# Decoder layer on one core: the second pass with three x buffers, the next x transposed ahead of the output product, squares within softmax, 32-row scores, and half of K and V made in the first row

## Chip, cores and metric

The kernel runs on one core of a Trainium2 chip. The metric is the device time of the program in microseconds (us). The engines are TensorE (PE; its weight loads are shown apart as PEld), VectorE (DVE), ScalarE (ACT), GpSimd (POOL) and SyncE (SP), which issues most of the DMAs.

## What is computed

A post-norm decoder layer on x of 8 x 512 x 512, all in fp32:

```
x = layernorm(x + mamba(x))                      # first pass, not touched by the change
q = x @ Wq.T + bq ;  k = ctx @ Wk.T + bk ;  v = ctx @ Wv.T + bv      # ctx: 8 x 77 x 512, 16 heads of 32
s = where(mask, -inf, q k^T / sqrt(32)) ;  x = layernorm(x + softmax(s) v @ Wo.T + bo)
xp = x shifted down by one token (zero first)
r = sigmoid((mu_r x + (1-mu_r) xp) @ Wr) ;  kk = relu((mu_k x + (1-mu_k) xp) @ Wk2)**2
x = layernorm(x + r * (kk @ Wv2))
```

## The kernel before

The program has two passes. The first (the Mamba block) writes x1 to device memory. The second, `cross_attention_ffn_pass`, is what the change edits. It is written for each engine by hand: every engine has its own list of instructions, in the order in which the code stands, and waits on counting semaphores. No scheduler moves anything.

The second pass works on the batch in 8 "rows" b of 512 tokens (T = 512 columns, four blocks `tb` of 128 tokens, four blocks `kt` or `j` of 128 features). Two rows are in flight: in the program's row b, the attention of row b and the feed-forward part (FFN) of row b-1 are woven together. TensorE runs, in this order:

- `front(b)`: 16 transposes of x (L1016) into `x1t`, then the query product (L1003, 16 matmuls of 128x512), with copies by ScalarE between;
- `scores(b, tb)` (L1042), four matmuls of 128x308 for each of the four token blocks. One matmul covers four heads: `kbd` holds the keys of a row as a block-diagonal matrix, 128 features by 4 x 77 keys, zero outside the blocks. Block j goes to PSUM bank 4+j, and VectorE takes each bank as soon as it is full (scale, mask, L1322), then a maximum (L1328) and, once GpSimd has subtracted it (L1410) and ScalarE has taken exp (L1206), the sum and its reciprocal (L1306 to L1311); GpSimd multiplies (L1415);
- between the four score blocks: `x2_transposes(b-1)` of the normed row b-1, and the FFN's `ffn_k` (L1003 with `xk`), which needs `mix`, VectorE's blend of x with its shifted copy (L1299; `mixed`);
- `ffn_r`, then `ffn_v` (L1009), which waits for `squared`: GpSimd squares `kf` (L1427) after the last of the softmax;
- `attend(b)`: 64 transposes of the probabilities (L1080) with ScalarE's copies, the values (L1067: four heads side by side, each in its own 32 columns of the array), and the output product (L1095). VectorE adds it to x (L1366) and takes the statistics; ScalarE makes the reciprocal deviation (L1188 Ln, L1190 Exp), VectorE the norm (L1340).

`x1t` is one buffer with three names (`kf = ot = x1t`): the transposed x, the FFN's squares, and the attended values. x lies in two buffers `xn`, by the parity of the row. PSUM banks 0 to 3 go round for products that ScalarE takes (`a_bank`), banks 4 to 7 for those of VectorE (`v_bank`): a product waits until the fourth before it has been taken.

Before the first row, all keys (L1106, 32 matmuls of 128x308) and values (L1114, 32 matmuls of 77x512) of the 8 rows are made. That set-up waits for one semaphore of six loads, the identity matrix the last of them.

Of the kernel before, what the change touches and what calls it, by code (L numbers as in the profile page):

```python
# [819 lines left out]
def cross_attention_ffn_pass(nc, x1, ctx_t, attn_mask, pad_mask, wq, wk, wv, wo, bq, bk, bv, bo,  # L820
# [28 lines left out]
    SETUP_A, SETUP_V = KT * (NB // KB), NB  # L849
    FRONT, FFN, ATTEND = 2 * KT, 3 * KT, NH + KT  # L850
# [3 lines left out]
    def front_a(b):  # L854
        return SETUP_A if isinstance(b, int) and b == 0 else b * ROW_A + (SETUP_A - FFN)
# [4 lines left out]
    def scores_v(b):  # L860
        return SETUP_V if isinstance(b, int) and b == 0 else b * ROW_V + (SETUP_V - TT)
# [7 lines left out]
    with ctx:  # L869
# [36 lines left out]
        top, total, live = (sb(n, [P, TT, NH]) for n in ("top", "total", "live"))  # L906
# [5 lines left out]
        kv_loaded = sem("kv_loaded")  # L912
        w_loaded = sem("w_loaded")
        x_loaded = [sem(f"x_loaded{i}") for i in range(2)]
# [41 lines left out]
        @block.sync  # L956
        def _(sp):
            def load(b, par):
                for tb in range(TT):
                    sp.dma_start(xn[par][:, tb, :], x1[b, tb * P:(tb + 1) * P, :]).then_inc(x_loaded[par], 16)  # L960

            def store(b, par):
                for tb in range(TT):
                    sp.wait_ge(normed3, b * TT + tb + 1)
                    sp.dma_start(out[b, tb * P:(tb + 1) * P, :], xn[par][:, tb, :]).then_inc(stored, 16)

            for dst, src in kv_loads:
                sp.dma_start(dst, src).then_inc(kv_loaded, 16)
            load(0, 0)
            for dst, src in loads:  # L970
                sp.dma_start(dst, src).then_inc(w_loaded, 16)

            def row(b, par):

                if isinstance(b, int) and b == 0:
                    load(1, 1)
                    return
                store(b - 1, 1 - par)
                if not (isinstance(b, int) and b == NB - 1):
                    sp.wait_ge(stored, b * (16 * TT))  # L980
                    load(b + 1, 1 - par)

            rows(row, sp)
            store(NB - 1, (NB - 1) % 2)
            sp.wait_ge(stored, NB * TT * 16)

        @block.tensor
        def _(pe):
            pe.wait_ge(kv_loaded, 16 * len(kv_loads))

# [29 lines left out]
            def front(b, par):  # L1020
                a = front_a(b)
                pe.wait_ge(x_loaded[par], (b - par) * (8 * TT) + 16 * TT)
                for kt in range(KT):
                    transposed(a, kt, xn[par])

                pe.wait_ge(a_taken, a + KT)
                for j in range(KT):
                    product_a(a, KT + j, lambda kt: wq_s[:, kt, j * P:(j + 1) * P], lambda kt: x1t[:, kt, :])

            def x2_transposes(b, a, par):  # L1030
                pe.wait_ge(normed2, b * TT + TT)
                for kt in range(KT):
                    transposed(a, kt, xn[par])
# [22 lines left out]
            def attend(b):  # L1056
# [30 lines left out]
                values(KT - 1, n)  # L1087

# [12 lines left out]
            for half in range(NB // KB):  # L1101
                for j in range(KT):
                    i = half * KT + j
                    a_bank(i + 1)
                    for kt in range(KT):
                        m = nc.tensor.matmul(ps[:, j, 0:KB * NK], wk_s[:, kt, j * P:(j + 1) * P],  # L1106
                                             ctx_s[:, kt, half * KB * NK:(half + 1) * KB * NK],
                                             start=(kt == 0), stop=(kt == KT - 1))
                    m.then_inc(a_filled, 1)

            for i in range(NB):
                v_bank(i + 1)
                for kt in range(KT):
                    m = nc.tensor.matmul(ps[0:NK, 4 + i % 4, :], ctx_s[:, kt, i * NK:(i + 1) * NK], wv_s[:, kt, :],  # L1114
                                         start=(kt == 0), stop=(kt == KT - 1))
                m.then_inc(v_filled, 1)
# [3 lines left out]
            def row(b, par):  # L1120
# [17 lines left out]
                if not first:  # L1138

# [3 lines left out]
                    ffn_v(b - 1, scores_v(b) + TT * KT)  # L1143
                attend(b)

            rows(row, pe)
            x2_transposes(NB - 1, LAST_A, (NB - 1) % 2)
# [8 lines left out]
        def _(act):  # L1156
            act.wait_ge(kv_loaded, 16 * len(kv_loads))
            act.wait_ge(zeroed, 2)
            for half in range(NB // KB):
                for j in range(KT):  # L1160
                    act.wait_ge(a_filled, half * KT + j + 1)
                    for i in range(HB):
                        r0 = i * DK
                        s = nc.scalar.activation(
                            kbd[r0:r0 + DK, half * KB:(half + 1) * KB, j, i * NK:(i + 1) * NK],
                            ps[r0:r0 + DK, j, 0:KB * NK].rearrange("p (b n) -> p b n", b=KB),
# [343 lines left out]
```

## Time and profile before

| | us |
|---|---|
| median of 3 runs | 2757.8 (2755.11 to 2761.13) |
| the profiled execution, its own time | 2748.2 |
| its span, first to last instruction | 2746.3 |
| set-up of the second pass starts on TensorE | 1854.42 |
| first output product (row 0) starts | 1959.38 |
| last output product (row 7) starts | 2661.13 |

TensorE is busy for 91% of the span, VectorE 71%, GpSimd 64%, ScalarE 53%. Most of VectorE's and GpSimd's time is the first pass. A matmul of fp32 shows as two instructions in the trace, each with its weight load, so 16 matmuls are "x32". The busy time of a group counts up to the end of its last instruction, which lies beside the start of the next group; the pace is read from one start to the next.

### The profile page before, as it was taken

How to read it: one execution, taken by the hardware profiler on the slowest of the kernel's cores; microseconds unless marked ns; L12 is line 12 of the kernel's file. 1: busy time of each engine (PE TensorE's matmuls, PEld its weight loads, DVE VectorE, ACT ScalarE, POOL GpSimd, SP SyncE). 2: the span in 40 equal slices, each digit the busy share in tenths (PEclk: the TensorE clock that was granted, in tenths of full speed). 3: DMA queues.
4: the chain of work that ended last, by engine and by line, in shares of the span. 5: the costliest groups of instructions: out<-in, count | busy, mean ns of one | idle time of the engine just before them, and what ended most of it. 6: DMA issues, size and time to landing. Idle time of an engine off the chain costs nothing. (4 is left out here: it accounts for less than half of the span.)

```text
span 2746.3 us, 37070 instructions
## 1 busy us (share of the span) xinstructions
PE 2496.2 (91%) x14848; PEld 1466.2 (53%) x14848; DVE 1963.0 (71%) x2273; ACT 1447.0 (53%) x2151; POOL 1765.5 (64%) x974
## 2 busy tenths in 40 slices
PE   7899999999999999999999997869799999999996
PEld 3566556556556555655565655534444444444443
DVE  3888997997998898888899798741456356446452
ACT  3576567567567557656657746513343343433432
POOL 0799889889889879878988988950333133124120
PEclk9999999999999999999999999989899999999998
DMA  3656666656766756665666675652000000000000
GB/s 136 154 124 138 175 136 135 181 129 134 185 131 140 186 111 149 140 166 130 148 176 133 128 169 124 135 135 109 0 0 31 31 0 31 31 25 7 31 16 16
DMA packets 99771, 292.11 MB, mean 106 GB/s; under 512 B 9360, under 2 KB 43664, under 8 KB 76944
## 3 DMA queue, kind: packets, MB, share of 16 engines
q0 software_dynamic: 27648, 167.78, 31.3%
q1 hardware_dynamic: 71952, 121.95, 12.6%
q8 instruction: 118, 1.93, 0.3%
q14 instruction: 53, 0.43, 0.1%
HBM read 104.89 MB, written 17.04 MB: 44 GB/s over the span
## 5 line engine op out<-in xcount | busy, mean ns | idle before, releaser
L781 POOL TENSOR_TENSOR mamba_ring<-mamba_ring,mamba_c_row 128x1024 f32<-128x1024 f32 x512 | 1286.9, 2586 | 177.7 <-DVE mamba_ring L664 176.3
L664 DVE TENSOR_TENSOR_SCAN mamba_ring<-mamba_ring,ps 128x512 f32<-128x512 f32 x1024 | 1177.0, 1201 | 149.0 <-PE ps L341 139.6
L535 ACT ACTIVATE mamba_ring<-mamba_delta,mamba_a_neg 128x512 f32<-128x512 f32 x1024 | 666.1, 712 | 468.3 <-DMA mamba_ring<-mamba_ring 335.2
L341 PEld LDWEIGHTS ps<-mamba_diag_b,mamba_v_t 64*128 64x128 f32 x8192 | 505.8, 190 | 365.9 <-issue 243.3
L341 PE MATMUL ps<-mamba_diag_b,mamba_v_t 64*128 64x128 f32 x8192 | 600.8, 288 | 89.0 <-DVE mamba_ring L664 87.9
L251 PE MATMUL ps<-mamba_xt,mamba_wu 128*128 128x512 f32 x512 | 254.9, 626 | 24.9 <-DMA mamba_wu<-w_u 12.9
L309 PE MATMUL ps<-mamba_xt,mamba_wres 128*128 128x512 f32 x512 | 256.5, 624 | 0.0
L1404 POOL TENSOR_TENSOR xf_xn<-xf_xn,xf_bo_s 128x512 f32<-128x512 f32 x32 | 39.7, 1274 | 333.1 <-PE xf_ps L1016 333.1
L364 PE MATMUL ps<-mamba_ident,mamba_ring 128*128 128x128 f32 x1536 | 189.8, 280 | 30.0 <-DMA mamba_ring<-mamba_ring 27.7
L1410 POOL TENSOR_TENSOR xf_pr<-xf_pr,xf_top 128x1232 f32<-128x1232 f32 x32 | 71.9, 2248 | 214.2 <-DVE xf_top L1328 214.2
L797 POOL DMA_DIRECT2D mamba_ring<-mamba_ring x192 | 174.4, 909 | 43.7 <-POOL mamba_ring L781 35.4
L642 DVE SCALAR_TENSOR_TENSOR mamba_u<-ps,mamba_wcv,mamba_u 128x511 f32<-128x511 f32 (+2 forms) x192 | 141.6, 738 | 73.1 <-ACT mamba_u L500 70.4
L364 PEld LDWEIGHTS ps<-mamba_ident,mamba_ring 128*128 128x128 f32 x1536 | 171.1, 144 | 42.3 <-DMA mamba_ring<-mamba_ring 22.4
L392 PE MATMUL ps<-mamba_wout,mamba_u 128*128 128x512 f32 x352 | 176.6, 621 | 0.0
L1003 PE MATMUL xf_ps<-xf_xk,xf_wkf 128*128 128x512 f32 x256 | 124.9, 646 | 28.3 <-DVE xf_xk L1299 21.6
L251 PEld LDWEIGHTS ps<-mamba_xt,mamba_wu 128*128 128x128 f32 x512 | 90.8, 195 | 108.6 <-issue 99.6
L773 POOL TENSOR_TENSOR mamba_v<-mamba_delta,mamba_u 128x512 f32<-128x512 f32 x64 | 96.2, 1503 | 62.2 <-ACT mamba_delta L517 62.2
L309 PEld LDWEIGHTS ps<-mamba_xt,mamba_wres 128*128 128x128 f32 x512 | 88.8, 193 | 76.1 <-issue 63.7
L500 ACT ACTIVATE mamba_u<-ps,mamba_bcv,mamba_wcv 128x512 f32<-128x512 f32 x64 | 49.5, 773 | 145.1 <-PE ps L251 145.1
L1322 DVE SCALAR_TENSOR_TENSOR xf_pr<-xf_ps,xf_mask 128x308 f32<-128x308 f32 x128 | 56.2, 471 | 96.7 <-PE xf_ps L1042 95.1
L1003 PE MATMUL xf_ps<-xf_x1t,xf_wq 128*128 128x512 f32 x256 | 113.8, 603 | 7.6 <-ACT xf_x1t L1176 7.6
L1232 ACT COPY xf_pt<-xf_ps 77x512 f32<-77x512 f32 x128 | 64.6, 593 | 105.9 <-PE xf_ps L1080 105.7
(111 smaller groups left out, 3050.7 us busy)
## 6 DMA issues: line engine op xcount, KB each, us to landing
mamba_ring<-mamba_ring POOLq DMA_DIRECT2D x128, 1024.0 KB, 7.6
mamba_c_row<-c_rows SPq DMA_DIRECT2D x32, 1024.0 KB, 10.2
mamba_ring<-mamba_ring POOLq DMA_DIRECT2D x64, 512.0 KB, 6.8
mamba_wu<-w_u SPq DMA_DIRECT2D x64, 256.0 KB, 3.5
mamba_wres<-w_res SPq DMA_DIRECT2D x64, 256.0 KB, 3.1
mamba_xt<-x_t SPq DMA_DIRECT2D x8, 1024.0 KB, 9.3
mamba_xres<-x SPq DMA_DIRECT2D x32, 256.0 KB, 9.1
x<-mamba_xres SPq DMA_DIRECT2D x32, 256.0 KB, 3.3
```

The costliest lines, as they stand in the source:

```text
L251: m = nc.tensor.matmul(ps[:, bank, :], wu[n % 2][:, kt, :], xt[b % 2][:, kt, :], start=(kt == 0), stop=(kt == KT - 1))
L309: m = nc.tensor.matmul(ps[:, BANK_B, :], wres[g % 2][:, kt, :], xt[b % 2][:, kt, :], start=(kt == 0), stop=(kt == KT - 1))
L341: m = nc.tensor.matmul(ps[:, 2 * s + i, tb * P:(tb + 1) * P], v_t[g % 2][i * H:(i + 1) * H, tb * P:(tb + 1) * P], diag_b[i * H:(i + 1) * H ...
L364: m = nc.tensor.matmul(ps[:, y_bank(g), tb * P:(tb + 1) * P], ring[:, r, i, tb * P:(tb + 1) * P], ident[:], is_transpose=True, start=(k == ...
L392: m = nc.tensor.matmul(ps[:, bank, :], u[b % 2][:, d, tb * P:(tb + 1) * P], wout[:, d, :], start=(d == 0), stop=(d == MOST[tb] - 1))
L535: a = nc.scalar.activation(ring[:, q % NR, i, :], delta[:, d, :], ACT.Exp, scale=a_neg[:, d, 2 * k + i:2 * k + i + 1])
L642: nc.vector.scalar_tensor_tensor(u[b % 2][:, j, lag:], ps[:, bank, 0:T - lag], wcv[:, j, TP - lag:TAPS - lag], u[b % 2][:, j, lag:], ALU.m ...
L664: m = nc.vector.tensor_tensor_scan(ring[:, r, i, :], ring[:, r, i, :], both[:, bass.ds(i, T, 2)], 0.0, ALU.mult, ALU.add)
L773: nc.gpsimd.tensor_tensor(v[:].rearrange("p b i t -> p i b t"), in_blocks(delta[:, d, :]), in_blocks(u[b % 2][:, d, :]), ALU.mult).then_in ...
L781: nc.gpsimd.tensor_tensor(ring[:, q % NR], ring[:, q % NR], c_row[:, 2 * k:2 * k + 2, :], ALU.mult).then_inc(c_done, 1)
L797: nc.gpsimd.dma_start(dst, src, accum_op=ALU.add).then_inc(merged[p], 16)
L1003: m = nc.tensor.matmul(ps[:, i % 4, :], lhs_t(kt), rhs(kt), start=(kt == 0), stop=(kt == KT - 1))
```

## The change

In the second pass alone:

- `xn` has three buffers (row b in `b % 3`), so x of row b+1 is there early; `kf = ot` is a buffer apart from `x1t`.
- `x1_transposes(b+1)` are issued within `attend(b)`, after the last values and before the output product.
- The query product of row b is split: two blocks, then the transposes of the normed row b-1, then the other two.
- Score blocks: 16 matmuls of K=32, 77 columns each, in the four 32-row tiles of the array, on plain keys `k_t` in place of the block-diagonal `kbd`. Head i of each block of four goes to bank 4+i, and the bank is full only when all four j are done.
- FFN products `ffn_k` 0, 1 after score block 0, 2, 3 after block 1; blocks 2 and 3 follow one another.
- GpSimd's squares lie within the softmax; VectorE's two `mix` are one place earlier; `live` and its product are one operation (L1340 of the new code).
- ScalarE loads one table for Ln and Exp ahead of its use, after the sigmoids; the deviation of the FFN's norm is made after the first four copies of `attend`.
- The keys of batch rows 4 to 7 are made between the score blocks of the first row, the values of 4 to 7 after them. The keys wait for three loads only.
- In the tail `ffn_k` waits for the first four of `mixed`, not for all.

The core of the diff:

```diff
-        kbd = sb("kbd", [P, NB, KT, HW])
+        k_t = sb("k_t", [P, NB, KT, NK])
-        xn = [sb(f"xn{i}", [P, TT, DM]) for i in range(2)]
+        xn = [sb(f"xn{i}", [P, TT, DM]) for i in range(3)]
-        kf = ot = x1t
+        kf = ot = sb("kf", [P, KT, T])
...
             def scores(b, tb):
                 v = scores_v(b)
                 if tb == 0:
-                    pe.wait_ge(a_taken, front_a(b) + 2 * KT)
+                    pe.wait_ge(a_taken, q_a(b, KT - 1) + 1)
                 for j in range(KT):
-                    v_bank(v + (tb * KT + j + 1))
-                    nc.tensor.matmul(ps[:, 4 + j, 0:HW], qt[:, j, tb * P:(tb + 1) * P], kbd[:, b, j, :],
-                                     start=True, stop=True).then_inc(v_filled, 1)
+                    for i in range(HB):
+                        r0 = i * DK
+                        if j == 0:
+                            v_bank(v + (tb * HB + i + 1))
+                        m = nc.tensor.matmul(ps[:, 4 + i, j * NK:(j + 1) * NK],
+                                             qt[r0:r0 + DK, j, tb * P:(tb + 1) * P], k_t[r0:r0 + DK, b, j, :],
+                                             start=True, stop=True, tile_position=(r0, 0))
+                        if j == KT - 1:
+                            m.then_inc(v_filled, 1)
...
                 values(KT - 1, n)
+                if b + 1 < NB:
+                    x1_transposes(b + 1)
...
+            for j in range(KT):
+                k_context(0, j)
+            pe.wait_ge(v_loaded, 16 * len(v_loads))
+            for i in range(VB):
+                v_context(i)
             pe.wait_ge(w_loaded, 16 * len(loads))
-            def row(b, par):
-                first = isinstance(b, int) and b == 0
-                front(b, par)
+            def row(b):
+                q_product(b, 0)
+                q_product(b, 1)
+                if b > 0:
+                    x2_transposes(b - 1)
+                q_product(b, 2)
+                q_product(b, 3)
                 scores(b, 0)
-                if not first:
-                    a = front_a(b) + FRONT
-                    x2_transposes(b - 1, a, 1 - par)
-                scores(b, 1)
-                if not first:
+                if b > 0:
+                    a = ffn_a(b - 1)
                     pe.wait_ge(mixed, (b - 1) * (2 * KT) + KT)
                     ffn_k(a, 0)
                     ffn_k(a, 1)
-                scores(b, 2)
-                if not first:
+                else:
+                    k_context(1, 0)
+                    k_context(1, 1)
+                scores(b, 1)
+                if b > 0:
                     ffn_k(a, 2)
                     ffn_k(a, 3)
+                else:
+                    k_context(1, 2)
+                    k_context(1, 3)
+                scores(b, 2)
                 scores(b, 3)
...
+                else:
+                    for i in range(VB, NB):
+                        v_context(i)
                 attend(b)
...
             x2_transposes(NB - 1)
-            pe.wait_ge(mixed, NB * (2 * KT))
+            pe.wait_ge(mixed, NB * (2 * KT) - KT)
             for j in range(KT):
                 ffn_k(LAST_A, j)
+            pe.wait_ge(mixed, NB * (2 * KT))
```

The order on TensorE, from the output product of one row to the FFN's `ffn_v` in the next; `xf_xn` transposed is x or the normed row, `xf_kbd` and `xf_k_t` are the keys. Before:

```order
L1095 MATMUL xf_ps<-xf_wo,xf_x1t 128x512 x16
L1016 MATMUL xf_ps<-xf_ident,xf_xn 128x128 x16
L1003 MATMUL xf_ps<-xf_x1t,xf_wq 128x512 x16
L1042 MATMUL xf_ps<-xf_kbd,xf_qt 128x308 x4
L1016 MATMUL xf_ps<-xf_ident,xf_xn 128x128 x16
L1042 MATMUL xf_ps<-xf_kbd,xf_qt 128x308 x4
L1003 MATMUL xf_ps<-xf_xk,xf_wkf 128x512 x8
L1042 MATMUL xf_ps<-xf_kbd,xf_qt 128x308 x4
L1003 MATMUL xf_ps<-xf_xk,xf_wkf 128x512 x8
L1042 MATMUL xf_ps<-xf_kbd,xf_qt 128x308 x4
L1003 MATMUL xf_ps<-xf_wr,xf_xr 128x512 x16
L1009 MATMUL xf_ps<-xf_wvf,xf_x1t 128x512 x16
```

And in the changed kernel, from the transposes that now stand ahead of the output product:

```order
L1014 MATMUL xf_ps<-xf_ident,xf_xn 128x128 x16
L1117 MATMUL xf_ps<-xf_wo,xf_kf 128x512 x16
L1000 MATMUL xf_ps<-xf_x1t,xf_wq 128x512 x8
L1014 MATMUL xf_ps<-xf_ident,xf_xn 128x128 x16
L1000 MATMUL xf_ps<-xf_x1t,xf_wq 128x512 x8
L1059 MATMUL xf_ps<-xf_k_t,xf_qt 128x77 x16
L1000 MATMUL xf_ps<-xf_xk,xf_wkf 128x512 x8
L1059 MATMUL xf_ps<-xf_k_t,xf_qt 128x77 x16
L1000 MATMUL xf_ps<-xf_xk,xf_wkf 128x512 x8
L1059 MATMUL xf_ps<-xf_k_t,xf_qt 128x77 x32
L1000 MATMUL xf_ps<-xf_wr,xf_xr 128x512 x16
```

The x transposes moved ahead of the output product, the normed ones into the query product, and two score blocks now stand together (x32) with nothing between.

GpSimd in one row, where `xf_top` is subtracted, `xf_total` multiplied, and the buffer of the squares is `xf_x1t` before:

```order
L1410 TENSOR_TENSOR xf_pr<-xf_pr,xf_top 128x1232 x2
L1415 TENSOR_TENSOR xf_pr<-xf_pr,xf_total 128x1232
L1410 TENSOR_TENSOR xf_pr<-xf_pr,xf_top 128x1232
L1415 TENSOR_TENSOR xf_pr<-xf_pr,xf_total 128x1232
L1410 TENSOR_TENSOR xf_pr<-xf_pr,xf_top 128x1232
L1415 TENSOR_TENSOR xf_pr<-xf_pr,xf_total 128x1232 x2
L1427 TENSOR_TENSOR xf_x1t<-xf_x1t 128x512 x4
```

The same engine and place in the changed kernel, with the squares on `xf_kf`:

```order
L1444 TENSOR_TENSOR xf_pr<-xf_pr,xf_top 128x1232 x2
L1449 TENSOR_TENSOR xf_pr<-xf_pr,xf_total 128x1232
L1455 TENSOR_TENSOR xf_kf<-xf_kf 128x512 x2
L1444 TENSOR_TENSOR xf_pr<-xf_pr,xf_top 128x1232
L1449 TENSOR_TENSOR xf_pr<-xf_pr,xf_total 128x1232
L1444 TENSOR_TENSOR xf_pr<-xf_pr,xf_top 128x1232
L1449 TENSOR_TENSOR xf_pr<-xf_pr,xf_total 128x1232
L1455 TENSOR_TENSOR xf_kf<-xf_kf 128x512 x2
L1449 TENSOR_TENSOR xf_pr<-xf_pr,xf_total 128x1232
```

All four squares now end one multiplication before the softmax does, in place of after it.

## Rows read from the trace of the kernel before

**Rows 1.** Windows: PE, PEld, DVE, ACT, POOL busy us; granted clock, DMA share, GB/s.
```profile
2250.00:2350.00 100.00, 94.97 (x325) 48.03 (x324) 52.17 (x91) 39.02 (x62) 28.01 (x17) 0.98 0.06 22
```

**Rows 2.** Timeline of TensorE, one steady row; start, us, operands, count [idle before].
```profile
2260.57 14.00 PE L1095 MATMUL xf_ps<-xf_wo,xf_x1t 128*128 128x512 f32 x32
...
2274.45 1.97 PE L1016 MATMUL xf_ps<-xf_ident,xf_xn 128*128 128x128 f32 x16
2277.25 14.00 PE L1003 MATMUL xf_ps<-xf_x1t,xf_wq 128*128 128x512 f32 x32 [0.83 <-ACT xf_x1t L1176]
2292.03 2.34 PE L1042 MATMUL xf_ps<-xf_kbd,xf_qt 128*128 128x308 f32 x8 [0.78 <-ACT xf_qt L1182]
2294.21 1.91 PE L1016 MATMUL xf_ps<-xf_ident,xf_xn 128*128 128x128 f32 x16
...
2301.28 8.83 PE L1003 MATMUL xf_ps<-xf_xk,xf_wkf 128*128 128x512 f32 x16 [3.09 <-DVE xf_xk L1299]
...
2335.19 14.00 PE L1009 MATMUL xf_ps<-xf_wvf,xf_x1t 128*128 128x512 f32 x32 [0.33 <-POOL xf_x1t L1427]
2349.03 3.66 PE L1080 MATMUL xf_ps<-xf_ident,xf_pr 128*77 128x128 f32 x32
...
2360.29 14.00 PE L1095 MATMUL xf_ps<-xf_wo,xf_x1t 128*128 128x512 f32 x32
```

**Rows 3.** Timeline of TensorE in the first pass: the two-tile products.
```profile
99.30 2.12 PE L341 MATMUL ps<-mamba_diag_b,mamba_v_t 64*128 64x128 f32 x32
...
704.86 1.16 PE L341 MATMUL ps<-mamba_diag_b,mamba_v_t 64*128 64x128 f32 x16
705.95 1.98 PE L309 MATMUL ps<-mamba_xt,mamba_wres 128*128 128x512 f32 x4
```

**Rows 4.** Timeline of VectorE and ScalarE in the steady row.
```profile
2278.83 1.28 ACT L1190 ACT_TABLE_LOAD   x1
...
2280.36 3.02 DVE L1340 TENSOR_SCALAR xf_xn<-xf_xn,xf_mv,xf_rstd 128x512 f32<-128x512 f32 x4 [1.90 <-ACT xf_rstd L1190]
...
2311.57 1.62 DVE L1322 SCALAR_TENSOR_TENSOR xf_pr<-xf_ps,xf_mask 128x308 f32<-128x308 f32 x4
```

**Rows 5.** Groups by line, second pass: busy, mean ns of one, idle before.
```profile
L1328 DVE TENSOR_REDUCE xf_top<-xf_pr 128x16 f32<-128x1232 f32 x32 | 46.0, 1436 | 1.1
L1410 POOL TENSOR_TENSOR xf_pr<-xf_pr,xf_top 128x1232 f32<-128x1232 f32 x32 | 71.9, 2248 | 214.2 <-DVE xf_top L1328 214.2
...
L1427 POOL TENSOR_TENSOR xf_x1t<-xf_x1t 128x512 f32<-128x512 f32 x32 | 32.4, 1039 | 71.1 <-ACT xf_x1t L1210 71.1
```

**Rows 6.** Timeline of TensorE from the set-up through the first row.
```profile
1854.42 18.63 PE L1106 MATMUL xf_ps<-xf_pt,xf_xr 128*128 128x308 f32 x64 [19.97 <-DMA xf_ident<-ident]
1872.89 27.63 PE L1114 MATMUL xf_ps<-xf_xk,xf_pt 128*77 128x512 f32 x64
...
1904.22 14.00 PE L1003 MATMUL xf_ps<-xf_x1t,xf_wq 128*128 128x512 f32 x32 [1.95 <-ACT xf_x1t L1176]
...
1946.05 5.74 PE L1080 MATMUL xf_ps<-xf_ident,xf_pr 128*77 128x128 f32 x32 [12.43 <-POOL xf_pr L1415]
...
1959.38 14.00 PE L1095 MATMUL xf_ps<-xf_wo,xf_x1t 128*128 128x512 f32 x32
```

**Rows 7.** DMA view and SyncE timeline: the key bias, last of the three loads for the keys.
```profile
xf_bk<-bk SPq DMA_DIRECT2D x1, 2.0 KB, 8.4
...
1841.99 0.42 SPq L968 DMA_DIRECT2D xf_bk<-bk  x1
```

**Rows 8.** Timelines of TensorE, VectorE and ScalarE after the last row.
```profile
2661.13 14.00 PE L1095 MATMUL xf_ps<-xf_wo,xf_x1t 128*128 128x512 f32 x32
...
2693.28 16.20 PE L1003 MATMUL xf_ps<-xf_xk,xf_wkf 128*128 128x512 f32 x32 [6.72 <-DVE xf_xr L1299]
...
2690.49 2.73 DVE L1299 SCALAR_TENSOR_TENSOR xf_xr<-xf_x2t,xf_omr,xf_xr 128x512 f32<-128x512 f32 x4
...
2739.75 1.28 ACT L1190 ACT_TABLE_LOAD   x1
```

More of the change, by code:

```diff
@@ L905, in cross_attention_ffn_pass @@
         tick = sb("tick", [P, 1])
-        top, total, live = (sb(n, [P, TT, NH]) for n in ("top", "total", "live"))
+        top, total = (sb(n, [P, TT, NH]) for n in ("top", "total"))
         st6, mv, rstd = sb("st6", [P, TT, 6]), sb("mv", [P, TT, 2]), sb("rstd", [P, TT])
@@ L1233, in attend @@
                         n += 1
+                    if j == 0 and before:
+                        rstd_ffn(b - 1)
                     if j >= 1:
@@ L1267, in _ @@
-            rows(row, act)
+                take_q(b, 0)
+                take_q(b, 1)
+                if b > 0:
+                    take_x2(b - 1)
+                    scale_x2(b - 1, xk, muk, range(KT))
+                take_q(b, 2)
+                if b > 0:
+                    scale_x2(b - 1, xr, mur, (0, 1))
+                take_q(b, 3)
+                if b > 0:
+                    scale_x2(b - 1, xr, mur, (2, 3))
+                else:
+                    take_context(1)
+                for tb in range(TT):
+                    exp(b, tb)
+                    if b > 0 and tb < 2:
+                        take_k(ffn_a(b - 1), 2 * tb)
+                        take_k(ffn_a(b - 1), 2 * tb + 1)
@@ L1268, in _ @@
+                if b > 0:
+                    for tb in range(TT):
+                        take_r(ffn_a(b - 1), tb)
+                    exp_tables()
+                attend(b, b > 0)
+            act.wait_ge(k_loaded, 16 * len(k_loads))
+            take_context(0)
+            act.wait_ge(w_loaded, 16 * len(loads))
+            act.wait_ge(consts, 5)
+            act.wait_ge(zeroed, 1)
+            exp_tables()
+            for b in range(NB):
+                row(b)
             rstd_of(z2_stats, 2 * TT, mv, rstd, rstd2_ln, rstd2, NB - 1)
-            take_x2(LAST_A)
@@ L1384, in _, with row @@
-            rows(row, dve)
-            last = (NB - 1) % 2
-            norms(NB - 1, last, mv, rstd, rstd2, normed2)
+            def row(b):
+                if b > 0:
+                    norms(b - 1, mv, rstd, rstd2, normed2)
+                softmax(b, b == 0)
+                if b > 0:
+                    ffn_out(b - 1, ffn_a(b - 1), scores_v(b) + TT * KT)
+                    norms(b - 1, gmv, grstd, rstd3, normed3)
+                attention_out(b)
+            for b in range(NB):
+                row(b)
@@ L1424, in squares @@
-            def squares(b, a):
-                for j in range(KT):
-                    pool.wait_ge(a_taken, a + (KT + j + 1))
-                    nc.gpsimd.tensor_tensor(kf[:, j, :], kf[:, j, :], kf[:, j, :], ALU.mult).then_inc(squared, 1)
-            def row(b, par):
-                first = isinstance(b, int) and b == 0
-                prepare(b, par)
-                softmax(b)
-                if not first:
-                    squares(b - 1, front_a(b) + FRONT)
-            rows(row, pool)
@@ new lines, in squares @@
+            def squares(b, js):
+                for j in js:
+                    pool.wait_ge(a_taken, ffn_a(b) + (KT + j + 1))
+                    nc.gpsimd.tensor_tensor(kf[:, j, :], kf[:, j, :], kf[:, j, :], ALU.mult).then_inc(squared, 1)
+            for b in range(NB):
+                prepare(b)
+                centre(b, 0)
+                centre(b, 1)
+                weigh(b, 0)
+                if b > 0:
+                    squares(b - 1, (0, 1))
+                centre(b, 2)
+                weigh(b, 1)
+                centre(b, 3)
+                weigh(b, 2)
+                if b > 0:
+                    squares(b - 1, (2, 3))
+                weigh(b, 3)
@@ L1440, in decoder_layer @@
+            squares(NB - 1, range(KT))
 def decoder_layer(nc, t, out):
```

292 lines of the change are left out of this document (131 added, 161 removed).

## The prediction

> **What bounds the kernel now.** I read the windows first: in 100 us of the steady part TensorE is busy for 94.97, VectorE for 52, GpSimd for 28 [rows 1]. So a row of the second pass lasts as long as TensorE's work plus its few waits, and another engine matters only where one of these waits ends on it. From one output product to the next a row takes 2360.29 - 2260.57 = 99.7 us [rows 2]; over the seven from row 0 to row 7 it is (2661.13 - 1959.38) / 7 = 100.25 [rows 6, 8].
>
> TensorE's timeline shows what the 99.7 hold [rows 2]. The big products pace at 13.8 us per 16 matmuls (2335.19 to 2349.03). The waits are: the copy of x before the query product (0.83 idle; with the pipeline's tail about 1.06 from the last transpose issued); the last copy of q before the scores (0.78, in the same way 1.05); VectorE's `mix` before `ffn_k` (3.09 idle, with the tail 3.3); the squares before `ffn_v` (0.33, some 0.5). The `mix` wait costs a second time: the 8 matmuls behind it take 8.83 against half of the 14.00 of a product of 16, because the granted clock falls to half behind that wait (0.98 on average over the window, rows 1); that is 1.8 us. A wait of 1.95 with no such loss stands before the first query product, which takes 14.00 [rows 6].
>
> **The change, part by part, in the steady row.**
> x of the next row is transposed before the output product, into a buffer of its own. The 16 transposes cost the same (1.97 with the tail, 1.74 of issue), but ScalarE's copies lie under 13.8 us of product: minus 1.06.
>
> `mix`: the transposes of the normed row now come 6.9 us into the query product instead of behind the first score block. Is the normed row ready? The norm starts at 2280.36, 6.0 behind the output product's end near 2274.4 [rows 2, 4]; 1.28 of that is a table load, now gone [rows 4]. Its four operations took 3.02 beside GpSimd's bias addition. That addition now lies under the output product, so I take 1.9 (the 2.7 of four larger VectorE operations with GpSimd idle, rows 8, is an upper bound). So ready at 4.7 + 1.9 = 6.6, against 6.9: no wait, or up to 0.9 if it stays at 3.0. From there to the blended `xk` is 7 us of copies, scalings and mix, at t = 14; `ffn_k` starts at 13.8 + 1.7 + 1.05 + 1.1 = 17.6. Minus 3.3 and minus the 1.8 of clock.
>
> Score blocks. Before, one takes 2.18 (2292.03 to 2294.21, rows 2), 2.07 of it products. The new one has 32 instructions of 77 columns. Its columns alone would need a quarter of the time of 308, divided once more among the tiles, so weight loads set the pace. The nearest rows are the two-tile products of the first pass, 64-row tiles and 128-column weights [rows 3]: 16 instructions take 1.09 to the next product's start, and 16 more add 2.12 - 1.16 = 0.96. That is 0.12 us for each pair side by side. If four row tiles load side by side as those two do, a block is 8 such steps, like those 16 instructions: 1.1. If only two do, it is 16 steps, 2.05; if none do, 32 steps, 3.84. I take 1.1: the tiles are apart in rows and banks as those two are, and the four value products of four heads (L1067) already run side by side in four column tiles. Four blocks: 4 x (1.1 - 2.1) = -4.
>
> A rule of the Trainium skill speaks against this (TensorE: Matmul & The Clock Gate, LDWEIGHTS): a weight load takes as long for 32 rows as for 128, since its columns count, 107 ns for 128 columns at 1.2 GHz. As an estimate from that page, 32 loads in turn would be 3.4 us a block, and nothing would be gained; the same page (Part 3) lets loads of different row groups overlap. The trace agrees with the first on the step's length (0.12) and with the second for two tiles; no row has four row tiles.
>
> A new wait: blocks 2 and 3 stand together, and a bank is full only at the block's end. Block 3 begins when VectorE has taken all four banks of block 2: 0.3 until the first starts, 1.6 for the four [rows 4], 0.1 back. Three quarters of block 3 remain behind the last bank, so it loses some 1.8. VectorE is free in time: block 1's maximum (1.44, rows 5) and shares end about 2 us before block 2 is full. Plus 1.8.
>
> Squares: they follow GpSimd's third multiplication. Counting on from block 2's take (t = 35.5): maximum 37, shares 39.8, block 3's take and maximum 42.9, subtraction 2.25 [rows 5], shares 45.5, multiplication 47.8, two squares of 1.04 [rows 5] 49.9. `ffn_v` is due at 36.5 + 13.8 = 50.3. Minus 0.5, but the margin is 0.4.
>
> ScalarE's reciprocal deviation within `attend` puts 0.6 among copies that TensorE waits for: plus 0.3. The wait of 1.05 before the scores stays. The other edits (`live`, three x buffers, loads two rows earlier) touch engines that wait anyway: nothing; without that cover `live` would be worth 1 us per block.
>
> The new row: five products 69.0, two sets of transposes 3.5, `attend` 11.3 (2349.03 to 2360.29) + 0.3, scores 4.4, waits 1.05 + 1.8 = 91.3. Seven rows, the last without transposes: 639.1 - 1.7 = 637.4 against 701.75: **minus 64**.
>
> **Set-up and row 0.** The keys need the first three loads: the last of them lands at 1841.99 + 8.4 = 1850.4 [rows 7], 3.8 before TensorE's start at 1854.42 [rows 6]. Half the keys: 64 instructions took 18.47, and at the 2.07 / 8 us of a score product of the same shape they would take 16.5, so 2.0 were lost to the clock's start at half: 8.2 + 2.0, to 1860.8. Four values at 27.6 / 8 = 3.43: 1874.5. From there to the query product 3.9 before, now with a table load of 1.28 ahead of the copies: 1879.7 (1904.22 before). Query product and wait to 1894.5; three score blocks and the other keys (2 x 4.1) to 1906. Here ScalarE can take exp 0 only after all the keys, at 1906; VectorE holds the take of block 2 behind its shares, until 1909.3. Block 3 ends at 1912, the first value product waits for a bank until about 1915, and by the 3.09 wait's example runs 1.8 slower: to 1930.6. `attend` and transposes 13.0: the output product starts at 1943.6 instead of 1959.38: **minus 15.7**. Of the 22 us of moved keys and values, most returns into this row, whose softmax left 12.43 idle [rows 6].
>
> **Tail.** `ffn_k` no longer waits for the four `xr` mixes, 2.7; two table loads (1.28 each, before norm 2 and before norm 3) are gone [rows 4, 8]: **minus 5.2**.
>
> Sum: 64.3 + 15.7 + 5.2 = 85, against a profiled execution of 2748.2 (span 2746.3 and 1.9 around it): 2663. The runs' median is 9.6 above that execution, so I forecast 2757.8 - 85 = **2672**.
>
> **Rivals.**
> Two tiles at a time (0.14): 32 blocks x 0.95 = 30 us back: 2702. For it: the only row-tile rows have two. Against it: the four column tiles.
> The clock falls in the thin stretch of blocks 2 and 3 too (0.13). For it: 2 us of tiled work around a 1.8 wait. Against it: a wait of 1.95 cost nothing [rows 6]. 1.8 to 3 in each of 7 rows: 2685 to 2693.
> `ffn_v` waits for squares, or the transposes for the norm (0.10): margins of 0.4 and 0.3. One to three us a row: 2679 to 2693.
> The tiles run in turn (0.05), the other side. Blocks of 3.84 give back 88: 2760, no change. The point is a block of 1.1 + 85 / 32 = 3.76; past it the kernel is slower, and if the half-busy array lets the clock fall as well, each block costs up to 7.7 and the time goes well over 2800. I give 0.02 to no change and 0.03 to slower.
> All as forecast (0.55): 2660 to 2686 for the small unknowns of 0 to 2 us a row. The rest (0.03) is faster, with blocks under 0.9 or a shorter row 0.
>
> **Numbers.** Time 2672. The range reaches from 2656 up to two tiles at a time, 2705; what lies outside is the tiles in turn and the ends. A measurement of this kernel tells some 0.2% (5.5 us) from no change. Faster than that: 0.95; within: 0.02; slower: 0.03.
>
> **What would show it.** A start-to-start pitch of 91 us between output products; no idle before the `xk` products and 7.0 us for their 8 matmuls; a score block of 1.1; one wait on VectorE's take (L1356) before block 3; no wait before `ffn_v`; the first output product near 1944 and TensorE's last score block of row 0 followed by a wait for a bank. The forecast is wrong if the weight loads of four row tiles don't overlap, since a third of the gain rests on that, or if the waits moved onto VectorE are longer than its own row's slack.

## The result, and the profile after

The changed kernel takes **2682.17 us** in the median (2679.95 to 2683.65, 4 runs) against 2758.72 for the kernel before beside it (2755.11 to 2761.13, 4 runs): a ratio of **0.9744**, 95% interval 0.9717 to 0.9771 (the ratio on record; these two medians alone give 0.9723). The forecast was 2672.

The profiled execution took 2683.6 (span 2681.8), 20.6 more than the 2663 of the forecast's sum. The first pass, which the change leaves alone, ran 4.0 longer in this execution (1840.65 against 1836.64 to the issue of its last four stores). I measure the second pass from there: 841.15 us against 909.68, **68.5 less**. That is 8 less than the 76.5 between the two medians, since the runs of the kernel before took some 10 us longer than its profiled execution (2748.2); in which part of the program these 10 us lie isn't on record.

| us | before | forecast | after |
|---|---|---|---|
| second pass to the first output product | 122.74 | 106.96 | 110.86 |
| seven rows | 701.75 | 637.4 | 651.18 |
| from the last output product on | 85.19 | 80.0 | 79.12 |

TensorE's timeline of a steady row, which answers to [rows 2]:

```profile
2231.60 13.90 PE L1117 MATMUL xf_ps<-xf_wo,xf_kf 128*128 128x512 f32 x32
2245.33 7.03 PE L1000 MATMUL xf_ps<-xf_x1t,xf_wq 128*128 128x512 f32 x16
2252.20 1.91 PE L1014 MATMUL xf_ps<-xf_ident,xf_xn 128*128 128x128 f32 x16
2253.95 7.03 PE L1000 MATMUL xf_ps<-xf_x1t,xf_wq 128*128 128x512 f32 x16
2261.75 1.13 PE L1059 MATMUL xf_ps<-xf_k_t,xf_qt 32*128 32x77 f32 x32 [0.78 <-ACT xf_qt L1200]
2262.82 7.13 PE L1000 MATMUL xf_ps<-xf_xk,xf_wkf 128*128 128x512 f32 x16
...
2278.00 1.13 PE L1059 MATMUL xf_ps<-xf_k_t,xf_qt 32*128 32x77 f32 x32
2279.69 2.27 PE L1059 MATMUL xf_ps<-xf_k_t,xf_qt 32*128 32x77 f32 x32 [0.55 <-DVE xf_pr L1356]
2281.88 15.70 PE L1000 MATMUL xf_ps<-xf_wr,xf_xr 128*128 128x512 f32 x32
2297.42 13.90 PE L1007 MATMUL xf_ps<-xf_wvf,xf_kf 128*128 128x512 f32 x32
```

Of the four waits of [rows 2], those for x, for `mix` and for the squares are gone; the one for q stays at 0.78. A score block takes 1.06 from start to start (2261.75 to 2262.82), half of the 2.18 before. The new wait is the 0.55 before block 3, and block 3 itself is stretched, since its banks come free one by one: from block 2's start to `ffn_r` it is 3.88 instead of 2 x 1.06, so 1.76 are lost. What the sum did not count stands in the next line: the 16 matmuls (x32) of `ffn_r` take 15.70, where `ffn_v` behind them takes 13.90. Windows around that place (PE, PEld, DVE, ACT, POOL busy; granted clock; DMA share; GB/s):

```profile
2278.00:2282.00 4.00, 3.45 (x66) 2.94 (x66) 2.81 (x5) 0.71 (x2) 3.10 (x3) 1.00 0.02 4
2282.00:2286.00 4.00, 4.00 (x6) 1.70 (x7) 3.93 (x8) 1.23 (x1) 3.27 (x2) 0.57 0.00 0
2286.00:2297.00 11.00, 11.00 (x27) 4.79 (x27) 6.93 (x9) 4.20 (x5) 9.89 (x6) 1.00 0.00 1
```

TensorE is busy throughout the second window, but at a granted clock of 0.57, near the lower of its two levels (1.2 of 2.4 GHz). In two of the seven rows the loss starts sooner, within block 3:

```profile
2465.30 3.02 PE L1059 MATMUL xf_ps<-xf_k_t,xf_qt 32*128 32x77 f32 x32 [0.55 <-DVE xf_pr L1356]
2468.24 16.57 PE L1000 MATMUL xf_ps<-xf_wr,xf_xr 128*128 128x512 f32 x32
```

The other engines in the first row shown, VectorE and GpSimd, against [rows 4, 5]:

```profile
2249.99 1.92 DVE L1377 TENSOR_SCALAR xf_xn<-xf_xn,xf_mv,xf_rstd 128x512 f32<-128x512 f32 x4 [0.60 <-ACT xf_rstd L1208]
...
2255.68 2.74 DVE L1331 SCALAR_TENSOR_TENSOR xf_xk<-xf_x2t,xf_omk,xf_xk 128x512 f32<-128x512 f32 x4 [3.38 <-ACT xf_xk L1220]
2231.84 4.94 POOL L1437 TENSOR_TENSOR xf_xn<-xf_xn,xf_bo_s 128x512 f32<-128x512 f32 x4 [29.27 <-PE xf_ps L1014]
...
2292.79 2.04 POOL L1455 TENSOR_TENSOR xf_kf<-xf_kf 128x512 f32<-128x512 f32 x2
```

The norm takes 1.92 (3.02 before); GpSimd's bias addition now lies 13 us ahead of it, and e3 below shows what it costs when the two overlap; the table load of [rows 4] before it is gone; `mix` ends at 2258.4, 4.4 before its reader. The last squares end at 2294.83, 2.6 before `ffn_v`.

TensorE in row 0, against [rows 6]:

```profile
1883.72 16.98 PE L1000 MATMUL xf_ps<-xf_x1t,xf_wq 128*128 128x512 f32 x32 [3.23 <-ACT xf_x1t L1195]
...
1916.46 3.13 PE L1059 MATMUL xf_ps<-xf_k_t,xf_qt 32*128 32x77 f32 x32 [3.03 <-DVE xf_pr L1356]
1922.06 16.55 PE L1045 MATMUL xf_ps<-xf_xk,xf_pt 128*77 128x512 f32 x32 [2.47 <-DVE xf_pr L1356]
```

The query product starts 43.07 into the second pass; the forecast's 1879.7 is 43.06. It then takes 16.98, 3.0 longer than the 14.00 of [rows 6].

### The profile page after: what moved, and what is told of

It is laid out like the page before. It is cut to its first block and busy times, and to the rows that moved or that the text cites. A ratio compares the mean times of both kernels' runs of the same rounds, so it can differ in the third digit from the quotient of the medians.

```text
span 2681.8 us, 38529 instructions
## 1 busy us (share of the span) xinstructions
PE 2475.2 (92%) x15616; PEld 1461.2 (54%) x15616; DVE 1942.1 (72%) x2241; ACT 1403.5 (52%) x2106; POOL 1755.6 (65%) x973
## 5 line engine op out<-in xcount | busy, mean ns | idle before, releaser
L1403 DVE TENSOR_TENSOR xf_xn<-xf_xn,xf_ps 128x512 f32<-128x512 f32 x32 | 21.2, 663 | 158.3 <-PE xf_ps L1117 158.3
L773 POOL TENSOR_TENSOR mamba_v<-mamba_delta,mamba_u 128x512 f32<-128x512 f32 x64 | 95.6, 1494 | 58.0 <-ACT mamba_delta L517 58.0
L1000 PE MATMUL xf_ps<-xf_wr,xf_xr 128*128 128x512 f32 x256 | 125.4, 653 | 0.0
L500 ACT ACTIVATE mamba_u<-ps,mamba_bcv,mamba_wcv 128x512 f32<-128x512 f32 x64 | 49.5, 773 | 145.0 <-PE ps L251 145.0
L1225 ACT ACTIVATE xf_pr<-xf_pr 128x1232 f32<-128x1232 f32 x32 | 39.3, 1230 | 162.1 <-POOL xf_pr L1444 162.1
L1000 PE MATMUL xf_ps<-xf_xk,xf_wkf 128*128 128x512 f32 x256 | 115.3, 605 | 4.1 <-DVE xf_xk L1331 4.1
```

The costliest lines, as they stand in the source:

```text
L1000: m = nc.tensor.matmul(ps[:, (a + i) % 4, :], lhs_t(kt), rhs(kt), start=(kt == 0), stop=(kt == KT - 1))
```

## The experiments

Each was timed in three rounds beside the kernel before (e1, e2, e5 and e8 on one chip, median 2751.5; e3, e4, e6 and e7 on one, 2751.0), the last two in five (2753.0). "Pitch" is the distance between the output products of neighbouring rows; the changed kernel's are 92.8 in four rows, 94.45 in two and 91.03 in the last, which has no x to transpose: 93.0 in the mean. Second pass and seven rows are from the profiled execution of each, in us. It is one of the runs, and in e1, e2, e3 and c1 the slowest of them (2737.91, 2668.85, 2701.05, 2687.70), so these two columns need not match the medians.

| run | median us | ratio (95%) | second pass | seven rows |
|---|---|---|---|---|
| e1_turn | 2726.92 | 0.9902 (0.9868 to 0.9936) | 882.69 | 689.19 |
| e2_apart | 2657.39 | 0.9637 (0.9602 to 0.9671) | 822.19 | 631.00 |
| e3_x1late | 2692.50 | 0.9775 (0.9727 to 0.9824) | 857.55 | 669.29 |
| e4_tables | 2719.98 | 0.9880 (0.9842 to 0.9918) | 873.79 | 680.30 |
| e5_squares | 2702.84 | 0.9804 (0.9777 to 0.9832) | 856.43 | 667.42 |
| e6_kvfirst | 2695.87 | 0.9790 (0.9753 to 0.9827) | 852.91 | 647.72 |
| e8_tiles_alone | 2749.15 | 0.9990 (0.9966 to 1.0014) | 903.37 | 696.42 |
| e7_best | 2654.52 | 0.9641 (0.9596 to 0.9686) | 809.99 | 625.29 |
| c1_changed | 2684.57 | 0.9746 (0.9723 to 0.9769) | 841.71 | 651.10 |
| c2_best | 2653.10 | 0.9642 (0.9625 to 0.9659) | 808.18 | 625.25 |

**e1_turn: the four row tiles one behind another.**

```diff
-                for j in range(KT):
-                    for i in range(HB):
+                for i in range(HB):
+                    for j in range(KT):
```

> The changed kernel, with the 16 score matmuls of a block in another order: all four of a head position (one row tile) behind one another, so that the four row tiles take turns in place of lying side by side. Theory (the four row tiles overlap their weight loads, and that is why a block takes 1.1 us): a block goes from 1.1 to about 32 x 0.12 = 3.8 us; block 3 no longer waits, as its first bank is free early, and the clock does not fall there, so a row grows by 4 x 2.7 less 1.8 less 1.8, about 7 us, eight rows about 58: 2740, range 2725 to 2765. Rival (a block is short since 77 columns are few, and order is nothing): a block stays at 1.1 and the time stays at 2682.

```profile
2291.83 3.36 PE L1059 MATMUL xf_ps<-xf_k_t,xf_qt 32*128 32x77 f32 x32 [0.78 <-ACT xf_qt L1200]
2295.12 9.74 PE L1000 MATMUL xf_ps<-xf_xk,xf_wkf 128*128 128x512 f32 x16
2304.79 2.65 PE L1059 MATMUL xf_ps<-xf_k_t,xf_qt 32*128 32x77 f32 x32
2307.36 7.13 PE L1000 MATMUL xf_ps<-xf_xk,xf_wkf 128*128 128x512 f32 x16
2314.43 6.01 PE L1059 MATMUL xf_ps<-xf_k_t,xf_qt 32*128 32x77 f32 x64
2320.37 15.93 PE L1000 MATMUL xf_ps<-xf_wr,xf_xr 128*128 128x512 f32 x32
```

A window of the same row, and lines of a shorter row:

```profile
2319.00:2321.00 2.00, 2.00 (x11) 1.73 (x10) 1.97 (x3) 0.00 (x0) 1.86 (x1) 0.50 0.00 0
...
1999.55 8.83 PE L1000 MATMUL xf_ps<-xf_xk,xf_wkf 128*128 128x512 f32 x16
...
2017.95 4.69 PE L1059 MATMUL xf_ps<-xf_k_t,xf_qt 32*128 32x77 f32 x64
2022.57 14.00 PE L1000 MATMUL xf_ps<-xf_wr,xf_xr 128*128 128x512 f32 x32
```

The same 32 instructions in another order take 2.57 instead of 1.06: 0.080 us each against 0.033. So the order counts, as it should if the tiles run side by side, and that is worth 1.5 a block. (The edit also puts four matmuls in a row into one PSUM bank; the two were not separated.) My price for "in turn" (3.84, from the 0.12 steps of two-tile pairs) was too dear. Weights of 128 columns loaded in turn would be 3.4 a block by the estimate from the Trainium skill (TensorE: Matmul & The Clock Gate, LDWEIGHTS); the 2.57 measured is below that too. Blocks 2 and 3 now run on without a wait, 6.01 for both here and 4.69 in the shorter row. The pitches alternate between 96.6 and 101.5 (the last is 94.8). Against the expectation the clock falls here too: in the longer rows twice, around block 0 (9.74 for the 7.13 of these 8 matmuls) and from within the last two blocks into `ffn_r` (15.93, granted clock 0.50); in the shorter ones only behind block 0 (8.83), and `ffn_r` takes 14.00.

**e2_apart: the first quarter of `ffn_r` (4 matmuls, x8 in the trace) between blocks 2 and 3.**

```diff
                 scores(b, 2)
-                scores(b, 3)
                 if b > 0:
                     pe.wait_ge(mixed, (b - 1) * (2 * KT) + 2 * KT)
-                    for tb in range(TT):
+                    ffn_r(a, 0)
+                scores(b, 3)
+                if b > 0:
+                    for tb in range(1, TT):
                         ffn_r(a, tb)
```

> The changed kernel, with score block 3 issued after the first quarter of the product ffn_r instead of right behind block 2 (rows 1 to 7). Theory (the miss of the forecast is the clock, which falls to half in the stretch of block 2, the wait and block 3): no wait before block 3 (1.8 us a row) and no slow ffn_r (1.8 to 2.8 us a row), 3.6 to 4.6 in all; but the squares, done about 1.0 us after ffn_v is then due, give 1 to 1.5 back: a row is 2.3 to 3.5 shorter, seven rows 16 to 24: 2662, range 2655 to 2668. Rival (the clock falls there because of the small products themselves, wherever they stand): ffn products after a block stay slow, only the wait of 1.8 less 1.2 is gained: 2678.

```profile
2273.03 1.13 PE L1059 MATMUL xf_ps<-xf_k_t,xf_qt 32*128 32x77 f32 x32
2274.09 3.70 PE L1000 MATMUL xf_ps<-xf_wr,xf_xr 128*128 128x512 f32 x8
2277.72 1.13 PE L1059 MATMUL xf_ps<-xf_k_t,xf_qt 32*128 32x77 f32 x32
2278.78 10.57 PE L1000 MATMUL xf_ps<-xf_wr,xf_xr 128*128 128x512 f32 x24
2289.91 14.00 PE L1007 MATMUL xf_ps<-xf_wvf,xf_kf 128*128 128x512 f32 x32 [0.56 <-POOL xf_kf L1457]
```

No wait, a block 3 of 1.06, and `ffn_r` at 3.70 + 10.57 for 4 + 12 matmuls: full speed in every row. The rival, that small products slow the clock wherever they stand, does not hold for a block of 1.06 by itself. The pitch is 90.40 throughout. From block 2's start to `ffn_v` it takes 16.88; in the changed kernel 19.42. Both missing terms go together: the 1.76 of block 3 and the 1.7 of clock, with about 0.9 given back, since TensorE now reaches `ffn_v` before GpSimd has the squares.

**e5_squares: all four squares after the last weighting.**

```diff
-                if b > 0:
-                    squares(b - 1, (0, 1))
...
-                if b > 0:
-                    squares(b - 1, (2, 3))
                 weigh(b, 3)
+                if b > 0:
+                    squares(b - 1, range(KT))
```

> The changed kernel, with GpSimd's squares back behind the last multiplication of the softmax. Theory (the squares within the softmax are worth more than the 0.5 us of wait that they had before, since ffn_v is now due earlier): the squares end 5.7 us later than now, 3.1 us after ffn_v is due, TensorE waits 3.1 us a row and runs 1.8 us of it again at half clock: seven rows add 22 to 34: 2710, range 2702 to 2718. Rival (as before the change, the squares cost 0.3 to 0.5 of wait): 2685.

```profile
2308.80 14.00 PE L1007 MATMUL xf_ps<-xf_wvf,xf_kf 128*128 128x512 f32 x32 [2.27 <-POOL xf_kf L1455]
...
2499.53 15.65 PE L1007 MATMUL xf_ps<-xf_wvf,xf_kf 128*128 128x512 f32 x32 [2.27 <-POOL xf_kf L1455]
```

The wait comes back as 2.27, less than the 3.1 expected, and the pitch is 95.37 in five rows, 2.5 more. In six of the seven rows no clock was lost behind the wait: the product takes 14.00. In one it takes 15.65, and that row's pitch is 97.01. So a wait of 2.3 behind a big product cost no clock in most rows and 1.65 in one, while the stretch of blocks 2 and 3, with a wait of only 0.55, cost clock in every row of this run too (`ffn_r` 15.52 to 16.82).

**e8_tiles_alone: the kernel before, with the 32-row scores alone** (the keys on `k_t`, one tile of 32 rows for each head, the loop of the changed kernel; nothing is reordered).

> The kernel before, with nothing changed but the scores: 32-row tiles on plain keys in place of the block-diagonal ones (and the two writes of keys that go with it). Theory (a block is 1.0 us shorter, but the block between the x2 transposes and the mix wait only lengthens that wait): three blocks of 1.0 a row, 3 us less, no new wait as the blocks stand apart, clock as before: seven rows 21 and row 0 about 1 to 3: 2736, range 2728 to 2742. Rival (score blocks are worth their whole 4 us a row): 2728 or less; rival (small products let the clock fall again): 2750 or more.

```profile
2293.21 1.13 PE L1045 MATMUL xf_ps<-xf_k_t,xf_qt 32*128 32x77 f32 x32
2299.50 8.79 PE L1003 MATMUL xf_ps<-xf_xk,xf_wkf 128*128 128x512 f32 x16 [5.16 <-DVE xf_xk L1301]
...
2332.68 14.00 PE L1009 MATMUL xf_ps<-xf_wvf,xf_x1t 128*128 128x512 f32 x32 [1.28 <-POOL xf_x1t L1428]
```

The blocks are 1.1 each and save 4 us a row, but the wait for `mix` grows from 3.09 [rows 2] to 5.16 and that for the squares from 0.33 to 1.28. The pitch falls by under 1 us and the time not measurably, so the 2736 expected was missed. About half of the longer `mix` wait is the block that no longer fills it; the other half is `mix` itself, 4.74 where it took 3.68 before, since more of it now falls beside GpSimd's subtraction (the last section has the line). The term "four blocks: minus 4" holds only together with the terms that remove the waits.

**e3_x1late: x transposed after the output product, as before.** `x1_transposes(b + 1)` moves from behind `values(KT - 1, n)` to behind the output product's loop; the three buffers stay.

> The changed kernel, with the transposes of the next x after the output product instead of ahead of it. Theory (all that the place is worth is the copy of x that it hides): the wait of 1.06 us before the query product is back, in seven rows: 7 to 8 us more, 2690, range 2686 to 2693. Rival (it also keeps GpSimd's bias addition away from VectorE's norm, and the transposes of the normed row would wait): a norm of 3.0 instead of 1.9, but due 2.8 later, so nothing more; if they waited all the same, 2698.

```profile
2253.94 7.13 PE L1000 MATMUL xf_ps<-xf_x1t,xf_wq 128*128 128x512 f32 x16 [0.83 <-ACT xf_x1t L1195]
...
2288.41 2.92 PE L1059 MATMUL xf_ps<-xf_k_t,xf_qt 32*128 32x77 f32 x32 [0.55 <-DVE xf_pr L1356]
```

VectorE's norm in the same row, and GpSimd's bias addition:

```profile
2255.86 3.95 DVE L1377 TENSOR_SCALAR xf_xn<-xf_xn,xf_mv,xf_rstd 128x512 f32<-128x512 f32 x4 [0.61 <-ACT xf_rstd L1208]
...
2253.19 5.13 POOL L1437 TENSOR_TENSOR xf_xn<-xf_xn,xf_bo_s 128x512 f32<-128x512 f32 x4 [43.06 <-PE xf_ps L1014]
```

The wait of 0.83 returns as in [rows 2]. The norm takes 3.95 instead of 1.92, since GpSimd's bias addition now runs beside it, but the transposes of the normed row come later as well and don't wait for it. The pitch is 95.6 in every row, 2.6 above the changed kernel's mean and not only 1.06: block 3 is in every row about as slow as in its two worst (2.92 here, 3.02 there), and against the pitch of those, 94.45, the difference is 1.15. But this execution (2701.05) is the slowest of four; the others took 2679.51, 2688.39 and 2696.61, at mean granted clocks of 0.975, 0.971 and 0.967 against its 0.966. One profile therefore can't say that the place of the transposes decides how much clock is lost at block 3. That the wait returns is shown; the difference in time from the changed kernel is not, for the intervals of the two ratios overlap.

**e4_tables: no explicit load of the joint table** (`pass` for `preload_act_table_set`).

> The changed kernel without the explicit table loads: ScalarE loads a table for Ln and another for Exp where they stand, as in the kernel before. Theory (the margin between the norm and the transposes of the normed row is 0.2 us, and the deviation within attend stands among copies that TensorE waits for): 1.3 us later norm gives 1.0 us of wait a row, two loads of 1.28 inside attend some 2.5 us a row: seven rows 25, tail 2.6: 2709, range 2697 to 2716. Rival (the loads are hidden as most of ScalarE's work is): 2685 at most.

```profile
2269.23 1.97 PE L1014 MATMUL xf_ps<-xf_ident,xf_xn 128*128 128x128 f32 x16 [0.88 <-DVE xf_xn L1377]
...
2334.60 1.06 PE L1087 MATMUL xf_ps<-xf_pt,xf_v_cur 77*32 77x512 f32 x8 [2.76 <-ACT xf_pt L1251]
2335.59 3.17 PE L1100 MATMUL xf_ps<-xf_ident,xf_pr 128*77 128x128 f32 x16
```

On ScalarE four loads of 1.28 a row stand where the changed kernel has its one explicit load. One delays the norm (wait 0.88), two stand within `attend` around the reciprocal deviation:

```profile
2330.87 1.28 ACT L1206 ACT_TABLE_LOAD   x1
...
2332.48 1.28 ACT L1208 ACT_TABLE_LOAD   x1
```

TensorE waits 2.76 there for copies of the probabilities, and the 16 transposes behind it take 3.17 instead of 1.97. Of these the expectation had only some 2.5, and at 2719.98 the time lies above its range. The seven rows are 29.1 longer, 4.2 each, and the tail 4.1 (83.25): in the new order, of which the deviation within `attend` is a part, the joint table carries nearly half of the 68.5.

**e6_kvfirst: all keys and values before row 0, as before.**

> The changed kernel with all keys and values made before the first row, as before the change. Theory (the moved half fills time in which row 0 waits for its softmax, so that only a part of its 22 us returns): the set-up is 22 us longer; row 0 takes, from its query product to attend, about the 42 us of the kernel before instead of 54.7: 9 us more in all: 2691, range 2685 to 2698. Rival (nothing of it is hidden): 2682. Rival (all hidden): 2704.

```profile
1951.56 6.55 PE L1100 MATMUL xf_ps<-xf_ident,xf_pr 128*77 128x128 f32 x32 [13.04 <-POOL xf_pr L1443]
```

Row 0's softmax leaves TensorE idle for 13.04, as the 12.43 in [rows 6], and the first output product comes 125.83 into the second pass instead of 110.86: the split of keys and values is worth 15.0 of the 68.5. The second pass as a whole is 11.8 longer, since the seven rows are 3.5 shorter: the first two have a pitch of 91.14, with no clock lost behind the same wait:

```profile
2015.61 2.27 PE L1059 MATMUL xf_ps<-xf_k_t,xf_qt 32*128 32x77 f32 x32 [0.55 <-DVE xf_pr L1350]
2017.81 14.00 PE L1000 MATMUL xf_ps<-xf_wr,xf_xr 128*128 128x512 f32 x32
```

So this place costs nothing, 1.7 or 3.3 by the row, in identical instructions.

**e7_best: what the losses suggest.** e2's order; squares 2 and 3 one place earlier; in row 0 the joint table ahead of the wait for the weights, and exp 0 ahead of the last two copies of keys.

```diff
+                if b > 0:
+                    squares(b - 1, (2, 3))
                 weigh(b, 2)
-                if b > 0:
-                    squares(b - 1, (2, 3))
                 weigh(b, 3)
...
-            take_context(0)
+            take_context(0, range(KT))
+            exp_tables()
             act.wait_ge(w_loaded, 16 * len(loads))
...
-            exp_tables()
```

> The changed kernel with block 3 apart as above, the last two squares between the fourth subtraction and the third multiplication, the table load of the set-up moved under the loads, and row 0's first exp ahead of the last two key copies. Theory: a row of 89.2 instead of 92.8 to 93.8 (no wait before block 3, no fallen clock, no wait for squares): 25 to 32 us; the set-up 1.3 shorter and its query product at full clock, 3; row 0 some 3: 2649, range 2642 to 2658. Rival (the squares or another wait take the place): the time of block 3 apart alone, 2662, or above.

> The changed kernel again, as the base of a comparison on one chip with the version below. Every theory: ratio 0.974 to 0.977 of the kernel before, a second pass of 841 us, pitches of 92.8 with one or two of 94.5, and block 3 behind a wait of 0.5 to 0.6 with the residual product at 15.7.

> The best version again beside the changed kernel. If the gain is in the second pass (block 3 apart, squares earlier, row 0's tables): 31 us less there than the changed kernel (810 against 841), pitches of 89.6 in every row, ratio 0.963 to 0.965 of the kernel before, so 0.988 to 0.990 of the changed kernel. If the 27 us between the two earlier medians came from different chips: less than 20 us apart here.

The steady row has no wait left but the 0.78 for q; here is one of its rows as a window of c2_best, which is the same kernel as e7_best:

```profile
2231.00:2320.00 89.00, 88.08 (x416) 44.81 (x415) 49.39 (x86) 34.23 (x58) 27.85 (x17) 1.00 0.07 24
```

TensorE is busy for 88.08 of 89 at a full clock (94.97 of 100 at 0.98 in [rows 1]). The pitch is 89.58. Side by side on one chip the best version takes 2653.10 and the changed kernel 2684.57, 0.988 of it (their intervals against the kernel before, 0.9625 to 0.9659 and 0.9723 to 0.9769, lie apart), and the second passes differ by 33.5: 25.9 in the seven rows, 7.1 before them. Most of that is already in e2: by time e2 (2657.39, its runs from 2652.30 to 2668.85) and e7 (2654.52) can't be told apart, and only the profiled second passes differ, by 12.2.

## Why the prediction came out as it did

**How near the number came, and by what.** The sum took 85 off and the second pass gave 68.5, some 17 less; yet the time is only 10 above the forecast. The other 6 or so are luck: the runs of the kernel before beside the changed one were slower than its profile, so the medians differ by 76.5. On the chip of c1_changed the same two kernels differ by 68.4 (2752.98 and 2684.57), what the profiles say. And 2682 lies among the times given to "all as forecast" (2660 to 2686), though what happened is the mechanism of the clock's rival, whose own times began at 2685.

**Held, term by term.** The sign, the mechanism and most terms hold. x ahead of the output product: its wait is gone, and returns in e3. `mix`: the norm at 1.92 for 1.9, no wait, no clock loss in `ffn_k`. Score blocks: 1.06 for 1.1; in e1, with the tiles in turn, 2.57. Block 3's wait: 1.76 for 1.8. Squares: done 49.5 after the end of the output product for 49.9; their margin of 2.6 is there because TensorE is late, and e2, which takes its losses away, shows the wait (0.56) that the forecast's margin of 0.4 warned of. Query product of row 0: 43.07 for 43.06. Tail: minus 6.1 for minus 5.2. (In the set-up's working the keys land 4.0 before TensorE's start by the figures given there, not 3.8; nothing hangs on the 0.2.)

**The term that failed.** "A new wait ... plus 1.8" counted the time but not the clock, which I had put among the rivals with 0.13. Against the 14.00 that `ffn_r` takes in e6's two rows without the loss, it cost 1.7 in five rows (15.70) and in the other two 3.3 (16.57 - 14.00, and 3.02 - 2.27 in block 3): 15 over seven rows. The rest of a row came out 0.2 better than the 91.3, so the seven rows are 13.8 over the forecast. e2 shows that it hangs on blocks 2 and 3 standing together: with 4 big matmuls between them, and the wait gone with that, no row of e2, e7 or c2 loses clock there. A wait between them isn't needed for it: in e1's longer rows they run on without one, and `ffn_r` is as slow (15.93). What precedes the fall in both is TensorE's work on small tiles: 3.88 with the wait here, 5.94 in e1. That these tiles are the cause, and not their place in the row, was not tested apart; and since e6 and e1 have rows without the loss, a forecast can only give it a share of the rows.

**The evidence against that rival was weak.** "A wait of 1.95 cost nothing" rested on one product [rows 6]. Behind the same wait, the same product in two executions of one kernel:

```profile
1885.27 15.70 PE L1000 MATMUL xf_ps<-xf_x1t,xf_wq 128*128 128x512 f32 x32 [1.95 <-ACT xf_x1t L1197]
```

in e7_best, and in c2_best:

```profile
1884.50 14.00 PE L1000 MATMUL xf_ps<-xf_x1t,xf_wq 128*128 128x512 f32 x32 [1.95 <-ACT xf_x1t L1197]
```

So it costs 1.7 or nothing, by the execution; one row could not decide it. e5 says the same of a wait of 2.27 (14.00 in six rows, 15.65 in one).

**Row 0, mis-sized by 3.9.** The table load before the copies of x made the wait 3.23 (1.95 before), as counted, but the query product behind it took 16.98 for the 14.0 assumed, and the values behind block 3, 3.05 late by then, 16.55 for 15.6. With the table loaded earlier (e7), the wait is 1.95 again. The clock in row 0 varies by execution: in c1_changed, the changed kernel again, that product took 15.48 behind 3.24. The remaining 4.0, in the first pass, is none of the change: its length varied from 1836.6 to 1853.4 over the profiles of all runs, with the same code.

**The side-by-side rivals.** Two tiles at a time (2702) and tiles in turn (2760) are both excluded by the 1.06. Had they run in turn, e1 says that the time would have been about 2727 and not 2760, since the step was dearer in my estimate (0.12) than it is (0.080) and block 3 no longer waits.

## What to carry to other kernels

When a change takes work off an engine that is 95% busy, ask at once what then stands together: shorter score blocks alone turned into longer waits (e8), and two blocks of small tiles with a short wait between them cost clock in the big product behind them in most rows, until four big matmuls stood between (e2). Price a new wait by the work around it as well as by its length, and don't take one row's clock as evidence for the next. A small piece of ScalarE work costs TensorE its whole length and more when it stands in front of a copy that is waited for: three table loads more a row, 3.8 us on ScalarE, cost 4.2 us of a row (e4), though ScalarE is busy for only about half of the time.

## What the hardware showed that I had not expected

- Instructions of 32 x 128 weights with 77 columns start every 0.033 us with the four row tiles side by side, and every 0.072 to 0.080 with four of one tile in turn (e1, 4.62 for 64 and 2.57 for 32): a factor of 2.2 to 2.4, not 4.
- The granted clock fell to 0.57 over 4 us though the only wait near was 0.55, and in e1 with none between the blocks; behind a wait of 2.27 (e5) it cost nothing in six rows of seven. The same instructions lost 0, 1.7 or 3.3 us by the row.
- VectorE's `mix` and norm are held up by a TENSOR_TENSOR of GpSimd beside them. The four `mix` operations take 2.74 when GpSimd is idle and 4.74 in e8, where the first of them alone takes 2.75 and the other three 0.7 each; GpSimd's one subtraction runs over that first one:

```profile
2294.71 2.75 DVE L1301 SCALAR_TENSOR_TENSOR xf_xk<-xf_x2t,xf_omk,xf_xk 128x512 f32<-128x512 f32 x1
2294.66 2.25 POOL L1411 TENSOR_TENSOR xf_pr<-xf_pr,xf_top 128x1232 f32<-128x1232 f32 x1 [14.25 <-DVE xf_top L1330]
```

The `mix` grew by 2.0 where GpSimd overlapped it for 2.2 (e8) and by 0.9 where it did so for 1.1 (before); the norm by 2.0 for 2.5 (e3) and by 1.1 for 1.1 (before). So VectorE gets little or nothing done in these two kinds of operation while GpSimd's lasts. Its addition from PSUM isn't slowed beside the same bias addition (0.66 in e3, 0.66 with GpSimd idle).
